# Diagonals summed on TensorE alone, and gated products released in halves, in a fused attention and mixture-of-experts kernel

## The reference, cut to what matters

```python
scores = einsum('bsqd,bskd->bsqk', qh, kh) / sqrt(8)      # 16 x 16 heads per token
scores = where(tril, scores, -1e18)
out    = einsum('bsqk,bskd->bsqd', softmax(scores), vh)
x  = x + tanh(g_xattn) * out(layernorm(x), ctx, ctx)
xf = layernorm(x)
logits = xf @ router_w.T + bias;  rw, sel = top_k(logits, 2);  rw = softmax(rw)
moe    = sum over the two experts e: rw_e * (silu(xf @ w1[e]) * (xf @ w3[e])) @ w2[e]
shared = (silu(xf @ sw1) * (xf @ sw3)) @ sw2
x  = x + tanh(g_ffn) * (moe + shared)
```

## Time and profile before

| | us |
|---|---|
| median of three runs | 604.19 |
| profiled execution | 603.94 |
| its span | 602.2 |
| VectorE busy | 489.9 (81%) |
| TensorE busy | 458.5 (76%) |
| GpSimd busy | 373.3 (62%) |
| ScalarE busy | 346.9 (58%) |

### The profile page before, as it was taken

How to read it: one execution, slowest core, us unless ns; L and a number is a source line. 1 busy time by engine, 2 the same in 40 slices (tenths; PEclk the granted TensorE clock), 3 DMA queues, 4 the chain that set the end, 5 groups by cost and what they waited for, 6 DMA issues and landing times.

```text
span 602.2 us, 11808 instructions
## 1 busy us (share of the span) xinstructions
PE 458.5 (76%) x3090; PEld 397.2 (66%) x3090; DVE 489.9 (81%) x1036; ACT 346.9 (58%) x1106; POOL 373.3 (62%) x370
## 2 busy tenths in 40 slices
PE   0064773880988887978986999798977999899950
PEld 0053442750877775868786988696766988899950
DVE  4999999799899998999987899988877744656541
ACT  5308629725875894399577865884274254355530
POOL 2100632288057888765877677878877776766762
PEclk9995895796599998999997999888997999999985
DMA  6501121013755286467534773389676495433496
GB/s 234 142 0 70 41 39 72 6 35 128 185 145 168 75 235 170 148 193 189 160 133 136 216 209 114 111 203 256 165 192 199 121 260 163 102 94 88 121 236 192
DMA packets 63408, 86.52 MB, mean 144 GB/s; under 512 B 10552, under 2 KB 38344, under 8 KB 63344
## 3 DMA queue, kind: packets, MB, share of 16 engines
q1 hardware_dynamic: 51600, 60.18, 34.3%
q0 software_dynamic: 11456, 25.59, 16.1%
q10 hardware_dynamic: 288, 0.00, 0.0%
HBM read 59.60 MB, written 26.71 MB: 143 GB/s over the span
## 4 chain that ended last, share of the span: by engine, by line
PE 29%; POOL 20%; DVE 14%; issue 11%; ACT 11%; DMA 7%; SPq 6%; POOLq 0%; DVEq 0%; ACTq 0%
POOL rows_in L707 12%; PE ps_g L1233 10%; PE ps_y L1266 7%; PE ps_g L1218 5%; ACT xn L1039 4%; DMA xr<-rows_in 3%; POOL rstd L682 3%; POOL ybuf L715 3%; DVE work L795 3%; DVE pv L827 3%; PE ps_o L1172 3%; DVE work L800 3%; DMA ybuf<-yr,xr 2%; SPq L572 2%; PE ps_r L1204 2%
## 5 line engine op out<-in xcount | busy, mean ns | idle before, releaser
L715 POOL DMA_INDIRECT ybuf<-yr,xr x149 | 158.8, 1066 | 70.2 <-issue 44.6
L707 POOL DMA_INDIRECT rows_in<-xn,idx x128 | 150.8, 1178 | 38.3 <-issue 37.4
L1233 PE MATMUL ps_g<-xrT,wq 128*128 128x128 f32 x1192 | 147.1, 279 | 0.4 <-ACT xrT L1115 0.4
L1266 PE MATMUL ps_y<-w2s,eo 128*128 (+1 forms) x852 | 120.5, 286 | 28.8 <-DVE eo L966 14.8
L1233 PEld LDWEIGHTS ps_g<-xrT,wq 128*128 128x128 f32 x1192 | 140.9, 195 | 1.7 <-issue 1.0
L1266 PEld LDWEIGHTS ps_y<-w2s,eo 128*128 128x128 f32 x852 | 109.4, 198 | 42.3 <-issue 38.1
L1108 ACT ACTIVATE sil<-ps_g 128x512 f32<-128x512 f32 (+1 forms) x108 | 63.5, 589 | 106.9 <-PE ps_g L1233 82.6
L966 DVE TENSOR_TENSOR eo<-sil,ps_g 128x512 f32<-128x512 f32 (+1 forms) x108 | 72.5, 672 | 41.4 <-ACT sil L1108 29.9
L795 DVE TENSOR_TENSOR work<-xn,ct 128x512 f32<-128x512 f32 (+21 forms) x144 | 93.8, 652 | 9.5 <-ACT xn L1039 5.6
L827 DVE TENSOR_TENSOR pv<-ex,ct 128x512 f32<-128x512 f32 (+21 forms) x144 | 89.3, 652 | 4.7 <-PE ps_o L1172 4.2
L800 DVE TENSOR_REDUCE work<-work 128x64 f32<-128x512 f32 (+21 forms) x144 | 92.8, 649 | 0.0
(11 more groups left out here) (107 smaller groups left out, 553.8 us busy)
## 6 DMA issues: line engine op xcount, KB each, us to landing
wq<-wall SPq DMA_DIRECT2D x104, 256.0 KB
xr<-rows_in SPq DMA_DIRECT2D x149, 65.0 KB, 2.5
xo<-ybuf POOLq DMA_DIRECT2D x10, 512.0 KB, 7.8
xt<-in_x SPq DMA_DIRECT2D x7, 512.0 KB, 3.9
ct<-in_ctx SPq DMA_DIRECT2D x7, 512.0 KB, 5.2
out<-xo SPq DMA_DIRECT2D x7, 512.0 KB, 4.4
xo<-x POOLq DMA_DIRECT2D x5, 512.0 KB, 6.2
ybuf<-yr,xr POOLq DMA_INDIRECT x149
```

The lines of the kernel that those rows point to most:

```text
L707: pool.indirect_dma_start(rows_in, bass.IndirectOffsetOnAxis(ap=idx[:, c % 2, k, t:t + 1], axis=0), xn2[:, c % XN, k, t], None).then_inc(s ...
L715: pool.indirect_dma_start(ybuf, bass.IndirectOffsetOnAxis(ap=xr_i[:, BLOCK[c, r + a] % XG, D + 1:DW], axis=0), yr[:, i % YR, a], None, bou ...
L1233: last = nc.tensor.matmul(ps_g[n % 2][:, q // HC, q % HC, a * P:(a + 1) * P], wq[:, b % WR, q * P:(q + 1) * P], xrT[:, i % 3, a * P:(a + 1 ...
L1266: last = nc.tensor.matmul(ps_y[:, a * D:(a + 1) * D], eo[:, n % 2, c, a * P:(a + 1) * P], w[:, c * D:(c + 1) * D], start=(c == 0), stop=(c ...
```

## The change

It has four parts. `ADDED` becomes empty for all chunks: line 835 no longer runs, and TensorE sums diagonals 1, 3, 5 and 7 too. The up products are issued half by half; a new semaphore `first` is raised when the gate half is complete, `gu` when the other half is. The SiLU waits for `first`, and for `eo` of pair n - 2; `eo` waits for the SiLU and for `gu`. TensorE waits for the SiLU of pair n - 2 before the gate half and for `eo` of pair n - 2 before the other half. The planner's model of these dependences is changed in the same sense, and its urgencies and tolerances are new, so every queue has another order.

```diff
-    ADDED = [[g for g in range(1, 8, 2)] if c > 1 else [] for c in range(CHUNKS)]
+    ADDED = [[] for c in range(CHUNKS)]
...
-               ('act', 'again'): 6.8, ('act', 'sil'): -7.1, ('act', 'xrT'): 2.6, ('act', 'yr'): 5.7,
-               ('pe', 'sums'): 7.1, ('pe', 'chain'): 7.7, ('pe', 'turn'): -12.0, ('pe', 'upR'): 7.7,
-               ('pe', 'upS'): 10.2, ('pe', 'down'): 3.8}
...
+               ('act', 'chain'): 7.2, ('act', 'again'): 11.2, ('act', 'sil'): 4.9, ('act', 'xrT'): 4.4,
+               ('act', 'yr'): 6.2, ('pe', 'sums'): 2.0, ('pe', 'chain'): 5.7, ('pe', 'turn'): 4.5,
+               ('pe', 'upR'): 8.1, ('pe', 'upS'): 9.6, ('pe', 'down'): 0.5}
...
-                deps = deps + waits(("eo", len(seq) - 2))
+                deps = deps + [(("eo", len(seq) - 2), HOP - .85), (("sil", len(seq) - 2), HOP)]
...
             def inner(n):
                 dve.wait_ge(s["sil"], n + 1)
+                dve.wait_ge(s["gu"], n + 1)
...
             def gated(n):
-                act.wait_ge(s["gu"], n + 1)
+                act.wait_ge(s["first"], n + 1)
+                need(act, s["eo"], n - 1)
...
             def up_routed(i):
-                if n >= 2 and not on_pe(("down", n - 2), ("upR", i)):
-                    pe.wait_ge(s["eo"], n - 1)
-                for a in range(w):
-                    b = BLOCK[c, r + a]
-                    need(pe, *((s["copied"], b - FROM + 1) if b >= FROM else (s_wq[b % WR], 16 * (b // WR + 1))))
-                    for q in range(2 * HC):
...
-                last.then_inc(s["gu"], 1)
+                need(pe, s["sil"], n - 1)
+                for half in range(2):
+                    if half and n >= 2 and not on_pe(("down", n - 2), ("upR", i)):
+                        pe.wait_ge(s["eo"], n - 1)
+                    for a in range(w):
+                        b = BLOCK[c, r + a]
+                        if half == 0:
+                            need(pe, *((s["copied"], b - FROM + 1) if b >= FROM else (s_wq[b % WR], 16 * (b // WR + 1))))
+                        for q in range(half * HC, (half + 1) * HC):
...
+                    last.then_inc(s[("first", "gu")[half]], 1)
```

More of the change, by code:

```diff
@@ L129, in planned @@
[L129 to L133, removed]
+        URG = {('sp', 'load'): 5.2, ('sp', 'result'): 8.7, ('sp', 'block'): 2.1, ('sp', 'zero'): 6.8,
+               ('sp', 'back'): 8.4, ('dve', 'ln1a'): -0.5, ('dve', 'scores'): 15.6, ('dve', 'values'): 2.0,
+               ('dve', 'sum'): 3.7, ('dve', 'chain'): -0.4, ('dve', 'slow'): 0.5, ('dve', 'eo'): -8.9,
+               ('dve', 'xo'): -1.7, ('dve', 'copy'): 5.3, ('dve', 'mix'): 6.3, ('dve', 'tab'): -1.2,
+               ('pool', 'inv1'): 2.2, ('pool', 'inv2'): 6.0, ('pool', 'scatter'): 3.3,
+               ('pool', 'post'): 10.7, ('pool', 'gather'): 2.2, ('act', 'nsum'): 14.2,
+               ('act', 'scaled'): 2.0, ('pool', 'residual'): 3.8, ('act', 'ln1b'): -1.2, ('act', 'exp'): 6.3,
+               ('act', 'chain'): 7.2, ('act', 'again'): 11.2, ('act', 'sil'): 4.9, ('act', 'xrT'): 4.4,
+               ('act', 'yr'): 6.2, ('pe', 'sums'): 2.0, ('pe', 'chain'): 5.7, ('pe', 'turn'): 4.5,
+               ('pe', 'upR'): 8.1, ('pe', 'upS'): 9.6, ('pe', 'down'): 0.5}
@@ L134, in planned @@
+        AHEAD = {'tr': 1.5, 'sil': 0.2, 'eo': 0, 'upR': 0, 'inv2': 0.8, 'scatter': 0.8, 'down': 0.2,
+                 'upS': 0.8, 'scores': 1.5, 'gather': 0.4, 'block': 0.4, 'chain': 0.2, 'turn': 0.4,
+                 'post': 0.8, 'back': 0, 'exp': 0.8, 'ln1b': 3.0, 'sums': 0.2, 'inv1': 1.5, 'sum': 0,
+                 'ln1a': 0.2, 'residual': 0.2, 'result': 3.0, 'values': 0, 'tab': 0, 'copy': 0.2,
+                 'slow': 0.4, 'xrT': 0.2}
         HOP = .15
@@ L512, in gated_attention_moe @@
                  "shift1 xn0 xn1 qk scatter_pause score mx sub exp sum rs pv o att x1 add xnt xntc xnc logit "
-                 "route d th share mask rank pos dest tab tabs zeroed sc0 sc1 gu sil eo y xt turned yev sh mix out halves sum0 sum1 mean0 mean1 sq0 sq1 ve0 ve1 scaled res").split()
+                 "route d th share mask rank pos dest tab tabs zeroed sc0 sc1 gu first sil eo y xt turned yev sh mix out halves sum0 sum1 mean0 mean1 sq0 sq1 ve0 ve1 scaled res").split()
         s = {n: sem("s_" + n) for n in names}
@@ L1214, in up_shared @@
                     pe.wait_ge(s["xntc"], HALVED[c + 1])
-                if n >= 2 and not on_pe(("down", n - 2), ("upS", j)):
-                    pe.wait_ge(s["eo"], n - 1)
-                for q in range(2 * HC):
-                    last = nc.tensor.matmul(ps_g[n % 2][:, q // HC, q % HC], ws[:, q * P:(q + 1) * P], xnT[:, c % XT, t:t + 2],
-                                            start=True, stop=True)
-                last.then_inc(s["gu"], 1)
+                need(pe, s["sil"], n - 1)
+                for half in range(2):
+                    if half and n >= 2 and not on_pe(("down", n - 2), ("upS", j)):
+                        pe.wait_ge(s["eo"], n - 1)
+                    for q in range(half * HC, (half + 1) * HC):
+                        last = nc.tensor.matmul(ps_g[n % 2][:, half, q % HC], ws[:, q * P:(q + 1) * P], xnT[:, c % XT, t:t + 2],
+                                                start=True, stop=True)
+                    last.then_inc(s[("first", "gu")[half]], 1)
             def up_routed(i):
@@ L1226, in up_routed @@
                     pe.wait_ge(s["turned"], i + 1)
-                if n >= 2 and not on_pe(("down", n - 2), ("upR", i)):
-                    pe.wait_ge(s["eo"], n - 1)
-                for a in range(w):
-                    b = BLOCK[c, r + a]
-                    need(pe, *((s["copied"], b - FROM + 1) if b >= FROM else (s_wq[b % WR], 16 * (b // WR + 1))))
[L1232 to L1236, removed]
+                need(pe, s["sil"], n - 1)
+                for half in range(2):
+                    if half and n >= 2 and not on_pe(("down", n - 2), ("upR", i)):
+                        pe.wait_ge(s["eo"], n - 1)
+                    for a in range(w):
+                        b = BLOCK[c, r + a]
+                        if half == 0:
+                            need(pe, *((s["copied"], b - FROM + 1) if b >= FROM else (s_wq[b % WR], 16 * (b // WR + 1))))
+                        for q in range(half * HC, (half + 1) * HC):
+                            last = nc.tensor.matmul(ps_g[n % 2][:, half, q % HC, a * P:(a + 1) * P],
+                                                    wq[:, b % WR, q * P:(q + 1) * P], xrT[:, i % 3, a * P:(a + 1) * P],
+                                                    start=True, stop=True)
+                    last.then_inc(s[("first", "gu")[half]], 1)
             which = {}
```

11 lines of the change are left out of this document (2 added, 9 removed).

## The result

The changed kernel takes 586.55 us (median of 4 runs, 583.90 to 589.34) against 605.51 us for the kernel before: ratio 0.9692, 95% interval 0.9652 to 0.9733. That is 3.1% faster, where 0.9% was forecast (598.3 from 603.94 us). So the profiles show 14.6 of the 19.0 us between the medians.

A forecast was written before the change was run, and what follows sets the result against it. It took VectorE to bound chunks 2 and 3, VectorE, TensorE and GpSimd together chunks 4 to 7, and TensorE the tail. 603.94 - 7.6 + 2 gave 598.3 us, forecast as 598, range 581 to 619.

The forecast's parts named there:

- Three signs: Expected in the trace: chunk 3's x1 at 181 us, chunks 4 to 7 about 61 us apart, line 827 waiting longer.
- the orders: New queue orders on all engines, taken as 0, with bounds -26 and +26 us from TensorE's waits at line 1180.
- Chunks 4 to 7: TensorE's 214.2 us of work gains 20.8 us of sums; +5 us, less 3 for the clock: net +2 us.
- GpSimd could give only 10.2 us: In chunks 4 to 7 GpSimd keeps its scatters and posts, so its 10.2 us of waits cap the gain.
- The end: Chunk 7's rows in DRAM, then TensorE's 90 us tail and 23 us of posting, reading back and storing: 0.
- Chunks 2 and 3: VectorE is the bound there, so dropping the additions comes off in full: -7.6 us.
- The halves: Earlier SiLU and `eo` in expert pairs, at most 8 us, already inside TensorE's raised busy share: 0.
- thirteen waits: TensorE's waits for `eo` between 150 and 489 us, at most 0.6 us saved in each: 8 us.
- The lock: VectorE's additions lock GpSimd's scatters out; without them an estimated 3 to 4 us less, costed at nothing.
- B: Rival: queues flow better, halving TensorE's waits at line 1180 and at `eo`; 588 us, chance 0.19.
- A: Rival: VectorE is the bound up to chunk 7 and TensorE absorbs the sums; 582 us, chance 0.14.
- C: Rival: TensorE becomes the bound at the sums in chunks 4 to 7, x1 5.2 us later in each; 620 us, chance 0.17.

The follow-up runs named there:

- a_adds: The changed kernel in its own orders with the 28 additions back on VectorE and TensorE summing twelve diagonals: 600.06 us.
- s_frozen: The kernel before in its old orders, with only the 28 additions moved from VectorE to sums on TensorE: 622.67 us.
- h_frozen: The kernel before in its old orders, additions still on VectorE, with only the halves put in: 602.43 us.
- b_both: The kernel before in its old orders, with both the sums on TensorE and the halves: 612.05 us.
- a_orders: The changed kernel's orders alone, with additions back on VectorE and up products released whole: 615.57 us.
- a_nohalves: The changed kernel in its own orders, with up products issued and released whole as before: 593.91 us.
- VectorE dose: Four score reductions a chunk done twice in chunks 2 to 7, 22.8 us in all: changed kernel 591.07 us, kernel before 611.14 us.

## Why the prediction was wrong

**The direction and the account of the engines held.** VectorE came out at 468.9 us busy where 465 was forecast, TensorE at 479.1 (485), at full clock and 96% busy in chunks 4 to 7 (93% or more). Three signs did not come: chunk 3 closes at 183.7 us (181 forecast), chunks 4 to 7 are 54.5 us apart (61), and line 827 waits for TensorE for 1.6 us in the whole run where it waited for 4.2, less and not more.

**The step that failed is the orders, costed at 0.** I gave them bounds of -26 and +26 us and took the middle, as if they were a part by itself. Measured with both other parts in place they are worth 4.3% (0.9692 / 1.0128), some 26 us, and without them they cost 1.7%. That this equals my bound of 26 us is luck: the bound was the wait at line 1180, and 16.4 of its 26.1 us lie in chunks 2 and 3, which got no shorter. In chunks 4 to 7 the wait fell by 4.5 us, a quarter of the idle time that went; the rest came mostly from TensorE's waits for `eo`, loaded rows, `yr` and the row copies. And 5.8 us came before chunk 2, in a stretch to which I gave nothing.

**Chunks 4 to 7, costed at +2 us, came to -25.6.** The step assumed that these windows contain a fixed amount of TensorE work, 214.2 us, to which 20.8 is added. The plan moved about 11 blocks out of them instead. Added up by estimate: 214.2 + 20.8 for the sums, less 16 for the blocks, less 9 for the clock (18.0 us of the busy time there was at the low clock, now none is; I had taken 3) is 210, and 208.1 was measured. The share was right, 95% forecast and 96% measured; the work was wrong. My argument that GpSimd could give only 10.2 us failed for the same reason: its instructions in the stage fell from 173 to 156, since posts moved along with the blocks. The time is given back where those blocks are worked: +12.2 us in the routing of chunk 7 and +4.1 behind it. A stage's load is not a constant when the order is free; the load of the run is.

**The end had another path.** I took it as the instant at which chunk 7's rows are in DRAM, plus 90 and 23 us. In the changed kernel the last chain holds no load of rows; TensorE's work sets it from 430.85 to 516 us. That fits with the 16.3 us which the moved blocks cost behind chunk 7. And the 91 us found for the tail is the length of a window, not a confirmation.

**Chunks 2 and 3, costed at -7.6 us, showed +0.5**, and yet the term was sized well: within the new orders the sums give -6.9 there (a_adds to the changed kernel). The new orders take it back in the same stretch, 108.5 us against 101.1 in a_adds and the kernel before. In the old orders the same shift lengthens the stretch to the close of chunk 3, from 188.97 us to 192.32 in s_frozen. Here the saving on the bounding engine came through only where the other engine's queue was arranged for what it takes over.

**The halves, costed at 0, give 0.7% in the old orders and 1.3% in the changed kernel**, 4 to 8 us. The bound of 8 us from the thirteen waits of the earlier trace rows was the right size for these two; with the additions in the new orders the halves give 2.9%, 17 us, twice the bound. Taking nothing of it was the error. Whether it is contained in the rise from 89 to 95%, as I said, these runs can't tell.

**The lock.** By the Trainium skill's rule (SBUF — State Buffer, "Who interferes with whom", there called the single rule) the additions kept GpSimd out, for an estimated 3 to 4 us. The runs agree in direction: the mean scatter is shorter without the additions in all four pairs of kernels that differ by them. In the old orders it falls from 1178 to 1090 ns (s_frozen) and from 1192 to 1108 (h_frozen to b_both), 11 us over 128 scatters; in the new ones from 1153 to 1115 (a_orders to a_nohalves) and from 1125 to 1109 (a_adds to the changed kernel), 5 and 2 us. No run isolates the lock from the shifted timing. The page of the changed kernel, for the earlier trace rows:

```profile
L707 POOL DMA_INDIRECT rows_in<-xn,idx x128 | 142.0, 1109 | 38.5 <-issue 38.5
```

That this shortens the run is not shown; s_frozen was slower.

**The rivals.** B had the right sign and 588 us, and its mechanism holds in part: the waits that it named shrank, at line 1180 from 43.5 to 31.4 us, but mostly where nothing was gained, and it knew nothing of the moved blocks. That its number is so near is partly luck. A, VectorE as the one bound, is refuted: a VectorE dose costs a third of itself. C is what happens in the old orders (620 forecast, 622.7 measured in s_frozen); its number was helped by errors that cancel, since chunks 2 and 3 took 2.9 us more there, not 7.6 less, and chunks 4 to 7 11.9 more, not 20.8.

**Open.** Which queue's new order carries the gain was not tried; only the combination is shown. Why both tuned sets of numbers are good is not reduced to a cause. The place of the inserted sums in s_frozen and of the additions in a_adds was mine, so a part of each cost may be that placement. The states with frozen foreign orders measure fit, not the best that each load could reach.

## What to carry to other kernels

When an order written out in advance goes with a change, treat order and load as one term: the same shift of work cost 2.7% in the old orders and gave 3.4% in the new. Predict the whole run by span = busy + rest of the engine nearest its limit, and ask which waits the new order can remove; don't hold a stage's work fixed if the order may move it to the next stage. Compare waits before and after by stage and not between fixed times, or a long wait falls out of one window and looks like a gain. And when a change is tried without making its order anew, or with an order tuned for other costs, a loss (here 16 to 26 us by the ratios) says little of the change.

## What the runs showed that I had not expected

Four plans made by the same planner from mismatched numbers all came out 3.5 to 4.3% slower than the kernel before, while one changed number, the rank of the sums, costs about 1% in either set. And TensorE's clock repaid part of the added sums: 33.7 us at full clock became 20.6 us of busy time, of which the clock explains an estimated 7, with the mean granted clock going from 0.902 to 0.922; in chunks 4 to 7 it went from 0.96 to 1.00 while the idle time there fell from 27.8 to 9.7 us.
